# Norms done tile by tile with low parts on GpSimd, and a sixth weight region, in a four-layer graph network on one core

## The reference, cut to what matters

```python
# layer 0: soft mixture, 64 experts of one slot, hidden size 192
logits = l2norm(x) @ (scale * l2norm(phi))      # 625 x 64
d, c = softmax(logits, over tokens), softmax(logits, over slots)
xs = d.T @ x                                    # 64 x 768
ys = gelu(xs @ w1[e] + b1[e]) @ w2[e] + b2[e]   # expert e sees slot e
x = x + c @ ys
# then, at the start of layer 1:
x_norm = layernorm(x); kqv = x_norm @ kqv_w.T + kqv_b
# layer 2, feed-forward: a narrow linear of 192 inputs ends in a norm and a router
x2 = x1 + gelu(h @ mlp_w1 + mlp_b1) @ mlp_w2 + mlp_b2
n = layernorm(x2) * ln2_g + ln2_b
scores = n @ gate_w.T + gate_b                  # 4 experts, top 2
```

## Time and profile before

| | |
|---|---|
| median of three runs | 2898.76 us (2897.23 to 2898.79) |
| the profiled execution | 2899.39 us, span of its trace 2897.3 us |
| mean granted TensorE clock | 0.979 |
| TensorE, VectorE, ScalarE, GpSimd busy | 94%, 49%, 39%, 24% of the span |
| HBM traffic | 215.00 MB read, 75 GB/s over the span |
| experts' weights | 64 DMAs of 576 KB (15.1 us to land) and 48 of 768 KB (20.5 us) |

### The profile page before, as it was taken

How to read it: one execution, slowest core, us unless ns; L and a number is a source line. 1 busy time by engine, 2 the same in 40 slices (tenths; PEclk the granted TensorE clock), 3 DMA queues, 4 the chain that set the end, 5 groups by cost and what they waited for, 6 DMA issues and landing times. The chain is left out here.

```text
span 2897.3 us, 49066 instructions
## 1 busy us (share of the span) xinstructions
PE 2711.2 (94%) x20003; PEld 2467.0 (85%) x20003; DVE 1418.9 (49%) x3603; ACT 1128.7 (39%) x2103; POOL 706.7 (24%) x261
## 2 busy tenths in 40 slices
PE   9999999998678999998899999999998999999899
PEld 9999999995337988998897999999668897797699
DVE  9777465664104135548752552241665563303743
ACT  7633255561003212327731253332563432356331
POOL 0144311110002331220224433323303431113032
PEclk9999999998898999999999999999999999999999
DMA  2022221015992211221021122222001221111022
GB/s 66 12 77 80 88 72 39 29 50 223 413 380 70 71 44 34 66 86 47 12 77 45 60 77 77 68 75 77 28 1 39 67 66 49 44 34 34 23 66 71
DMA packets 164572, 220.08 MB, mean 76 GB/s; under 512 B 21801, under 2 KB 144325, under 8 KB 164350
## 3 DMA queue, kind: packets, MB, share of 16 engines
q1 hardware_dynamic: 164350, 216.95, 22.6%
HBM read 215.00 MB, written 1.92 MB: 75 GB/s over the span
## 5 line engine op out<-in xcount | busy, mean ns | idle before, releaser
L58 PE MATMUL ps<-weights_r,buf_r 128*125 128x256 f32 (+3 forms) x4110 | 545.7, 285 | 5.8 <-DVE kv L2830 1.7
L279 POOL TENSOR_TENSOR weights_r<-weights,head_weights_r 128x1536 fp32r<-128x1536 f32 (+2 forms) x80 | 276.2, 3453 | 1040.2 <-ACT head_weights_r L272 1007.8
L58 PEld LDWEIGHTS ps<-weights_r,buf_r 128*125 128x125 f32 (+1 forms) x4110 | 516.3, 187 | 9.1 <-issue 4.2
L279 POOL TENSOR_TENSOR weights_r<-weights,weights_r 128x1536 fp32r<-128x1536 f32 x76 | 269.5, 3545 | 974.0 <-ACT weights_r L272 974.0
L58 PE MATMUL ps<-xT_r,weights_r 128*128 128x376 f32 (+4 forms) x2028 | 333.8, 309 | 0.0
L58 PE MATMUL ps<-head_weights_r,buf_r 128*125 128x256 f32 (+2 forms) x2250 | 309.8, 284 | 0.0
L58 PEld LDWEIGHTS ps<-xT_r,weights_r 128*128 128x128 f32 (+1 forms) x2028 | 303.2, 189 | 3.2 <-issue 2.2
L58 PEld LDWEIGHTS ps<-head_weights_r,buf_r 128*125 128x125 f32 x2250 | 287.5, 188 | 0.0
L58 PE MATMUL ps<-weights_r,xT_r 128*125 128x256 f32 x1680 | 233.4, 282 | 8.2 <-issue 4.8
L58 PEld LDWEIGHTS ps<-weights_r,xT_r 128*125 128x125 f32 x1680 | 212.9, 186 | 10.6 <-issue 5.4
L272 ACT ACTIVATE head_weights_r<-weights 128x1536 fp32r<-128x1536 f32 (+2 forms) x80 | 114.8, 1435 | 254.7 <-PE ps L58 134.5
(11 more groups left out here) (383 smaller groups left out, 4322.1 us busy)
## 6 DMA issues: line engine op xcount, KB each, us to landing
expert_regions<-in_L_ffn_w SPq DMA_DIRECT2D x64, 576.0 KB, 15.1
expert_regions<-in_L_ffn_w SPq DMA_DIRECT2D x48, 768.0 KB, 20.5
weights<-in_L_mix_fc_w SPq DMA_DIRECT2D x24, 768.0 KB, 4.5
weights<-in_L_gnn_W SPq DMA_DIRECT2D x18, 768.0 KB, 4.6
weights<-in_L_ffn_W SPq DMA_DIRECT2D x12, 768.0 KB, 4.7
weights<-in_L_mix_w_mapT SPq DMA_DIRECT2D x9, 768.0 KB, 5.0
weights<-in_L_gnn_W_out SPq DMA_DIRECT2D x9, 768.0 KB, 4.6
weights<-in_L_mix_kqv_wT SPq DMA_DIRECT2D x9, 768.0 KB, 4.6
```

The costliest lines, as they stand in the source:

```text
L58: mm = net.nc.tensor.matmul(ps, net.r(stationary(s, k)), net.r(moving(m, k)), start=(n == 0 and k == 0), stop=(stop and n == 2 and k == kc ...
L279: self.nc.gpsimd.tensor_tensor(self.r(load.dst), load.dst, self.r(load.high), ALU.subtract).then_inc(self.low_made, 1)
```

## The change

The arena gets a region `edges` of 4696 elements, on which counts and mask now lie, and which is the sixth region of the experts; `DEPTH` becomes 6. `KeepCounts` stores the counts to DRAM once they are final; the region is fetched when the last heads of layer 0 are done and the store has landed; the counts are loaded back after the last turn of `SlotSecond`, and `Degrees` moves behind the query linear. `PairedNorm` takes any number of units and loads and a place for the low parts. The slots' norm and the narrow linear's norm use it with `lows="gpsimd"`: without columns ScalarE then makes a plain copy of the turned tile beside the high part, and GpSimd subtracts; the last tile's low parts stay on VectorE. The query linear and the gate router get `prior`. In all norms of the class the split of the next weights moves ahead of the last tile.

```diff
-        sizes = dict(xT=BUF, ..., weights=(WSLOTS + 1) * SLOT)
+        sizes = dict(xT=BUF, ..., weights=(WSLOTS + 1) * SLOT, edges=NT * N + 3 + 1568)
+        self.counts = nc.alloc_sbuf_tensor_at("edge_counts", [128, NT, N], F32, offset=at - 4 * sizes["edges"])
+        self.mask = nc.alloc_sbuf_tensor_at("edge_mask", [128, NT, N], BF16, offset=at - 4 * sizes["edges"] + 4 * (NT * N + 3))
+        self.counts_kept, self.kept = nc.dram_tensor("counts_kept", (TP, NT * N), F32, kind="Internal").ap(), sem("counts_kept_landed")
-        self.counts = sb("edge_counts", [128, NT, N])
-        self.mask = sb("edge_mask", [128, NT, N], BF16)
@@ LinearT.tensor
-                pe.wait_ge(*self.tiles[2 if self.prior and j == 0 else 3 if j == 0 else 4])
+                for t in (2,) if self.prior and j == 0 else (3,) if j == 0 else (3, 4):
+                    pe.wait_ge(*self.tiles[t])
@@ PairedNorm.__init__
+        last, halves, pair = NT - 1, (0, 1), NT * (len(units) - 2)
+        self.weights = [load for load in dict.fromkeys(u["load"] for u in units) if isinstance(xT, Pair)]
+        self.copied = lows == "gpsimd" and not columns
+        changes = lambda t: 3 if columns else int(self.copied and t < last)
+        lowered = lambda t: [("low", t, g) for g in halves] if lows == "vector" else []
+        for i in range(pair):
+            pe.append(("product", i))
+            dve += [("add", i), ("moments", i)]
         for t in range(NT):
+            pe += [("product", pair + t), ("product", pair + NT + t)] + [("turn", t - 1, g) for g in halves if t > 0]
...
             act.append(("root", t))
-            if t == 0:
-                act.append(("weights", 1))
+            if t == 0 and len(self.weights) > 1:
+                act.append(("weights", len(self.weights) - 2))
             if t > 0:
                 act += [q for g in halves for q in columned(t - 1, g)]
+                pool += [("low", t - 1)] if lows == "gpsimd" else []
+        dve += lowered(last - 1)
+        if self.weights:
+            act.append(("weights", len(self.weights) - 1))
         if columns:
             act += columned(last, 0)
...
-        act.append(("weights", 2))
@@ PairedNorm.gpsimd
+        for load in self.weights[2:]:
+            self.net.split_low(load.unit, load.segment)
+        for load in self.weights[1:2]:
+            self.net.split_low(load.unit + 2, load.segment)
+        for _, t in self.order["pool"]:
+            ts = slice(t * TP, (t + 1) * TP)
+            hi, lo = (x[:, :, ts] for x in (self.outT.hi, self.outT.lo))
+            self.wait(pool, "act", "high", t, 1)
+            self.nc.gpsimd.tensor_tensor(self.net.r(lo), lo, self.net.r(hi), ALU.subtract).then_inc(self.net.pool.sem, self.net.pool.one())
+        for load in self.weights[2:] or self.weights[:1]:
             self.net.split_low(load.unit + 2, load.segment)
@@ 
+class KeepCounts:
+    def sync(self, sp):
+        for sem, value in self.made:
+            sp.wait_ge(sem, value)
+        for p0, p1 in ((0, 112), (112, TP)):
+            sp.dma_start(self.net.counts_kept[p0:p1], self.net.counts[p0:p1].rearrange("p t n -> p (t n)")).then_inc(self.net.kept, 16)
-    EXPERTS, GROUP, DEPTH, TILES = 64, 4, 5, 3
+    EXPERTS, GROUP, DEPTH, TILES = 64, 4, 6, 3
@@ network
+    KeepCounts(net, loops.ends())
...
+            FirstFetches(net, ins["L0_ffn_w1"], (5,), attended + [(net.kept, 32)])
...
-    normed = LinearNorm(net, units[0]["xT"], units, R, tok(G[2]), XT, 1e-5)
+    normed = PairedNorm(net, units[0]["xT"], units, R, tok(G[2]), XT, 1e-5, lows="gpsimd")
...
-    degrees = Degrees(net, rdeg)
-    made = linear_T(net, XT, w, feat(G[0]), bias=col["kqv_b_c"][:, 0:6], cols=(0, D), tiles=normed.made)
+    made = linear_T(net, XT, w, feat(G[0]), bias=col["kqv_b_c"][:, 0:6], cols=(0, D), tiles=normed.made, prior=normed)
     square = Square(net, feat(G[0]), feat(G[1]), made, start)
+    counts = net.into(None, None, second.ends()[:1])
+    counts.pieces = [(net.counts[p0:p1].rearrange("p t n -> p (t n)"), net.counts_kept[p0:p1]) for p0, p1 in ((0, 112), (112, TP))]
+    counts.value, counts.before.used_at = 16 * len(counts.pieces), (queries, 2)
+    degrees = Degrees(net, rdeg, counts, start)
...
-    normed = linear_norm(net, hT, ins["L2_ffn_mlp_w2"], ..., kp=96, ...)
+    normed = paired_norm(net, hT, ins["L2_ffn_mlp_w2"], ..., kp=96, ..., lows="gpsimd")
-    scored = router(net, XT, ins["L2_ffn_gate_wT"], ..., tiles=normed.made)
+    scored = router(net, XT, ins["L2_ffn_gate_wT"], ..., tiles=normed.made, prior=normed)
```

More of the change, by code:

```diff
@@ L1136, in __init__ @@
         self.scale, self.rstd = net.st[:TP, 70:75], net.st[:TP, 186:191]
-        self.order = {e: [] for e in ("pe", "act", "dve")}
-        pe, act, dve = (self.order[e] for e in ("pe", "act", "dve"))
-        last, halves = NT - 1, (0, 1)
-        columned = lambda t, g: [("column", t, g, c) for c in range(3 if columns else 0)] + [("high", t, g)]
-        for t in range(NT):
-            pe.append(("product", t))
-            dve += [("add", t), ("moments", t)]
-        for t in range(NT):
-            turned = [("low", t - 2, g) for g in halves] if t > 1 else []
-            pe += [("product", NT + t), ("product", 2 * NT + t)] + [("turn", t - 1, g) for g in halves if t > 0]
-            dve += [("add", NT + t), ("moments", NT + t)] + (turned if t == last else []) + [("add", 2 * NT + t), ("moments", 2 * NT + t), ("mean", t)]
+        self.order = {e: [] for e in ("pe", "act", "dve", "pool")}
@@ L1177, in __init__ @@
                 net.freed[b] = (ticks.sem, self.at[engine]["column", q[1], q[2], 2])
+            elif self.copied and q[1] < last:
+                net.freed[b] = (net.act.sem, self.at["act"][("high",) + q[1:]])
             else:
                 net.freed[b] = (net.dve.sem, self.at["dve"][("low",) + q[1:]])
-        self.made = [(net.dve.sem, self.at["dve"]["low", t, 0 if columns and t == last else 1]) for t in range(NT)]
+        self.made = [(net.pool.sem, self.at["pool"]["low", t]) if ("low", t) in self.at["pool"] else
+                     (net.dve.sem, self.at["dve"]["low", t, 0 if columns and t == last else 1]) for t in range(NT)]
         self.take(**{e: len(seq) for e, seq in counted.items()})
@@ L1275, in scalar @@
         nc, done, mv = self.nc, self.net.act, self.net.mv
-        self.net.split_high(self.weights[2].unit, self.weights[2].segment)
+        for load in self.weights[2:]:
+            self.net.split_high(load.unit, load.segment)
         for q in self.order["act"]:
@@ L3361, in vector @@
         self.begin(dve)
+        self.landed(dve)
         done = self.net.dve
@@ L3917, in network @@
     landing = [net.into(biases[1][p:p + 4, :], ins["L2_ffn_exp_b2"], clear.ends()) for p in (0, 32)]
[L3918 to L3919 removed]
+    normed = paired_norm(net, hT, ins["L2_ffn_mlp_w2"], X, tok(G[0]), XT, 1e-5, [norm_cols[n] for n in ("L2_ffn_ln2_g", "L2_ffn_ln2_b")], kp=96,
+                         after=now() + bias_out.ends(), tiles=shared.tiles_done(), lows="gpsimd")
     start = now()
     halves = SplitRows(net, biases[1], biases[0], landing)
[L3922 removed]
+    scored = router(net, XT, ins["L2_ffn_gate_wT"], logits[:, :, 0:4], net.row(ins["L2_ffn_gate_b"]), tiles=normed.made, prior=normed)
     chosen = TopTwo(net, logits, gates, "top", sel, None, scored)
```

53 lines of the change are left out of this document (29 added, 24 removed).

## The result

The changed kernel takes 2907.59 us (median of nine runs, 2901.84 to 2912.30), the kernel before 2898.14 us in the runs beside it (nine, 2894.44 to 2904.46). The ratio is 1.0026, with a 95% interval of 1.0017 to 1.0035. It isn't the quotient of the two medians, which is 1.0033; in all that follows the two differ by up to 0.07%, or 2 us. Forecast were 2892.8 us and a range up to 2898.0. The profiled execution of the changed kernel is the longest of its nine: 2912.30 us, span 2910.4, mean granted clock 0.972 (before: span 2897.3, clock 0.979). Over its nine runs the clock's median is 0.976.

What follows compares the result with a forecast made beforehand. TensorE, busy 94% of the span, bounds the kernel, so only its waits count. Terms -5.7 + 1.8 - 2.6 - 0.6 + 1.1 = -6.0 us from 2899.39 give 2893.4; the median, 0.63 lower, 2892.8; range 2887.0 to 2898.0.

Steps and rivals of the forecast that it cites:

- Step 5: Next weights' split before the last tile: -0.6 us at the experts' router, +1.1 us for both norms with columns.
- step 3: Slots' norm tile by tile, low parts on GpSimd: first query linear product +1.0, last tile's turn +0.8, together +1.8 us.
- Exclusion, slower: Rival: low parts on GpSimd hold up the norm each time in slots' and narrow norms; 2906.8 us, chance 0.04.
- Step 1: Sixth region for the experts' weights, filled beforehand: one refill fewer, 88 DMAs instead of 92, -5.7 us.
- Step 2: Counts kept in DRAM and reloaded, degree sum behind the query linear: landed when VectorE asks, 0 us.
- Step 4: Narrow linear's norm: router's first piece 5.5 us earlier, second 4.0 or 1.3, experts' products follow; -2.6 us.
- the -3.4 us: The prediction's sum if the narrow norm gained nothing, moving work between VectorE and GpSimd being no help.

Runs made afterwards that it cites:

- experiment 3: Changed kernel, early weights' split kept, but in the two norms with columns GpSimd waits for VectorE's last low part before its split; 2897.17 us, ratio 0.9995.
- experiment 2: Kernel before with only the next weights' split on ScalarE moved ahead of the last tile; 2906.04 us against 2899.53, ratio 1.0026.
- experiment 5: Changed kernel with the next weights' split back behind the last tile only in the two norms with columns; 2893.33 us, ratio 0.9981.
- experiment 10: Changed kernel, but in the norms with columns VectorE makes the last half's high part by three operations from PSUM; 2901.81 us, ratio 1.0016.
- experiment 12: Kernel of experiment 9, but GpSimd's second split of the query linear's weights waits for the slots' first norm; 2891.83 us, ratio 0.9977.
- experiment 6: Kernel of experiment 1 with the small split of the experts' bias rows issued behind layer 2's router instead of ahead; 2893.80 us, ratio 0.9984.
- experiment 1: Changed kernel with the next weights' split back behind the last tile in every tile-by-tile norm; 2894.16 us, ratio 0.9984.
- experiment 4: Kernel before with the sixth region alone, counts stored and loaded back, degree sum behind the query linear; 2893.93 us against 2899.53, ratio 0.9986.
- experiment 9: Experiment 5 and experiment 7 together, plus the bias rows' split behind the choice of the experts; 2892.30 us, ratio 0.9974.
- experiment 7: Kernel of experiment 1 with the slots' first-half products and adds all ahead, only the second half tile by tile; 2891.49 us, ratio 0.9976.

## Why the prediction was wrong, step by step

**Step 5 failed.** It said: "the last half's high part is made 1.47 later, of which 1.0 lies beside VectorE's own half, so the second pieces, already 0.56 late at 1696.69, start 0.5 later", +1.1 us for both norms. It priced ScalarE's order and never asked where the GpSimd half of the moved split would land. The 0.5 is right (experiment 3). The term left out is GpSimd's 3.44 us on top of a VectorE copy of 0.42: 3.3 us of stall in each norm and the clock behind it, 6.1 and 4.8 us in the traces instead of 0.5 each. The description of `LinearNorm` ahead of the prediction said that the last tile's second half is done on VectorE, and step 3 had the mechanism from a norm of 3.13 us. The rule was applied to the new GpSimd work only, not to the old work that moved. At the router the swap was worth 0.3 us in experiment 2 and 0.2 in experiment 5, not 0.6, since ScalarE's split waited for its weights. In the changed kernel's profile the clock fell there too (0.52 from 1145 to 1155, before 0.91), which is most of the +2.5 of the table. Over the router's second piece it fell in three of the nine profiled kernels with the swap there (the changed one, experiments 10 and 12) and in none of the five without, though in two of those just behind it (the kernel before, experiment 6). TensorE stands 1.8 to 2.0 us before the piece with the swap and 1.3 to 1.5 without; that this brings the clock down isn't shown. Experiment 5 keeps that swap and lost nothing by its median.

**The rival "Exclusion, slower"** had the right mechanism and nearly the right time (2906.8), and a chance of 0.04. It had the wrong place: it looked for the collisions in the two new norms, where they cost at most 1 us a time. The loss isn't in these stages, as experiments 1 and 4 show.

**Step 1 was right**: 88 DMAs instead of 92, -5.75 us at the first add, and -5.6 by the medians of experiment 4. Only the time of the sixth region's fetch was off: it went out at 584.10, not at 632, which changed nothing. **Step 2 was right**: no wait at the degree sum. **Step 3 was right**: first norm 3.11 us and VectorE idle 5.2 us before its root (said 4.9), tiles 3.60 apart, GpSimd's low part 1.78 (said 1.8), first linear product 24.33 us after the first add (said 24.6). It cost 1.65 us by the products' starts (said 1.8). Luck has a part in that agreement: against experiment 4, which has the old norm, it is 2.7 us, and the old norm itself varies by 1.0 between the two profiles with the clock.

**Step 4 was right up to its last sentence.** The router's first piece came 22.24 us after the first product (said 22.3), with norms 2 and 4 held. The second piece came 1.3 us earlier in the changed kernel, the value given for the lower clock, and 2.5 in experiment 1, between the two. But the -2.6 needs "The experts' products follow the router", and there it failed: 34.26 us after the first add against 34.03, and 0.6 less in experiment 1. In the changed kernel the second piece itself ran at the lower clock and took back what it had gained (0.72 and 1.00, six products in 1.42 and 0.85). At the full clock, in experiment 1, the eviction of the scores stands behind a held split of bias rows, and the gates' transposes follow a VectorE queue that experiments 6 and 9 shortened in vain. It was worth 0, not 2.6, and the -3.4 us that the prediction set beside its sum for that case was right on this term.

By the products' starts the terms are -5.75 + 1.65 + 0, and 6.1 and 4.8 for the norms with columns: +6.8 us. The profiled executions differ by 13.1. The rest, 6.3, is 2.5 at layer 1's router and 3.8 in small steps elsewhere, most of them at the lower clock. By the medians the loss is 9.45.

## What to carry to other kernels

When a step is moved, follow every engine's part of it to where it lands, not only that of the engine whose list is edited: ask which VectorE operation between SBUF and SBUF will run beside the GpSimd part. A held operation costs the whole rest of GpSimd's instruction, here up to 3.4 us for one of 0.4, so long GpSimd instructions belong where VectorE reads PSUM or has nothing due. And a wait that is taken away is only worth what the next one leaves: follow the chain on to the next long stretch of TensorE before counting it.

## What the runs showed of the hardware

A GpSimd operation on SBUF holds back to its end a VectorE copy within SBUF (0.42 to 3.61 us), a tensor-scalar within SBUF (0.68 to 3.11) and a tensor-tensor with both inputs in SBUF (two in 3.26 instead of 1.01). It doesn't hold operations that read PSUM (three in 1.03 either way), nor the adds from PSUM that ran beside the split in experiment 7 (0.54 at 873.13, as ever). The Trainium skill says so in "SBUF — State Buffer", section "Who interferes with whom": a VectorE instruction with two SBUF inputs contends with a GpSimd instruction that reads SBUF, and one in a two-port mode takes part in the lock; the trace of experiment 10 agrees (1.03 and 3.26). Not every operation within SBUF is held: the statistics (`BATCH_NORM_STATS2` of 125x384, 0.56 us) and the inverses (`RECIPROCAL` of 125x1, 0.16) take as long beside a split as without one, in experiment 7 at 872.66 and in the changed kernel at 874.34. It works in the other direction as well: in experiment 12 GpSimd's low part, which began while a VectorE norm ran, took 2.11 us instead of 1.78.

The mean granted clock differs between executions of one kernel about as much as between kernels: 0.972 to 0.977 in nine runs of the changed kernel, 0.974 to 0.980 in ten of experiment 10, 0.978 to 0.982 in eleven of experiment 1, and 0.975 to 0.981 in twelve of the kernel before, beside experiments 1 to 4. The profiled execution of the changed kernel has the lowest clock of its nine (0.972), that of experiment 10 the highest of its ten (0.980). So one profile's clock says little of its kernel; clear of it is only that all runs of the changed kernel lie below all of experiment 1. A gain of 1 to 2 us at one place was several times not seen in the median, and no run tells why.
